# Output projection of an attention kernel: seven block products per slot in place of eight

## What is computed

```python
x = x + 0.5 * ffn(layernorm(x))
x = x + attn(layernorm(x))
x = x + 0.5 * ffn(layernorm(x))
# attn, shortened
q = rms_norm(x @ wq_a.T, q_norm_w) @ wq_b.T            # 32 heads, 128 + 64 (rotary)
kv_up = rms_norm(kv_c, kv_norm_w) @ wkv_b.T            # k_nope and v of each head
scores = (q_nope . k_nope + q_pe . k_pe) * scale       # causal
probs = softmax(scores)
out = (probs @ v).reshape(b, s, 32 * 128) @ wo.T
```

## Time and profile before

| | us |
|---|---|
| median of 3 runs (2258.32 to 2260.1) | 2259.83 |
| span of the profiled execution | 2257.3 |
| TensorE busy | 2213.3 (98%) |
| TensorE weight loads busy (beside the matmuls) | 1871.3 (83%) |
| VectorE busy | 1594.8 (71%) |
| ScalarE busy | 968.0 (43%) |
| GpSimd busy | 576.2 (26%) |

### The profile page before, as it was taken

How to read it: one execution, slowest core, us unless ns; L and a number is a source line. 1 busy time by engine, 2 the same in 40 slices (tenths; PEclk the granted TensorE clock), 3 DMA queues, 4 the chain that set the end, 5 groups by cost and what they waited for, 6 DMA issues and landing times.

```text
span 2257.3 us, 39455 instructions
## 1 busy us (share of the span) xinstructions
PE 2213.3 (98%) x11932; PEld 1871.3 (83%) x11932; DVE 1594.8 (71%) x3663; ACT 968.0 (43%) x2441; POOL 576.2 (26%) x642
## 2 busy tenths in 40 slices
PE   8989999999999999999999999999999999999998
PEld 7978888888888888887788988888888888888887
DVE  7656667776676766777787666766777766666777
ACT  6543444443444443443465534334344443334344
POOL 5312222122221222212144332222222222222212
PEclk9999999999999999999999999999999999999999
DMA  4023333332233333333423123333323333333321
GB/s 161 15 72 114 113 113 103 113 86 87 76 103 110 111 113 112 104 108 105 154 86 98 44 77 83 82 82 82 81 80 81 82 82 82 82 82 82 79 71 75
DMA packets 217433, 207.09 MB, mean 92 GB/s; under 512 B 144288, under 2 KB 172832, under 8 KB 215328
## 3 DMA queue, kind: packets, MB, share of 16 engines
q1 hardware_dynamic: 196928, 162.32, 25.7%
q10 hardware_dynamic: 20448, 44.04, 5.8%
HBM read 101.45 MB, written 54.53 MB: 69 GB/s over the span
## 4 chain that ended last, share of the span: by engine, by line
PE 88%; DVE 5%; issue 2%; DMA 2%; ACT 1%; POOL 1%; SPq 0%; ACTq 0%; DVEq 0%; POOLq 0%
PE ps L777 69%; PE ps L1141 6%; PE ps L856 4%; PE ps L1085 2%; PE ps L791 1%; PE ps L803 1%; DVE stage L2029 1%; DVE arena L1692 1%; PE ps L1092 1%; PE ps L1123 1%; ACT arena L1303 1%; DVE negmax L2019 1%; PE ps L805 1%; PE ps L1119 1%; DVE stats L1701 0%
## 5 line engine op out<-in xcount | busy, mean ns | idle before, releaser
L777 PE MATMUL ps<-arena 128*128 128x512 f32 x3264 | 876.9, 404 | 8.9 <-DVE xacc L1794 4.9
L1692 DVE TENSOR_TENSOR arena<-ps,arena 128x512 fp32r<-128x512 f32 (+2 forms) x920 | 538.4, 597 | 414.2 <-ACT arena L1303 414.0
L1303 ACT ACTIVATE arena<-ps 128x512 fp32r<-128x512 f32 (+2 forms) x920 | 471.8, 525 | 656.8 <-PE ps L777 429.6
L777 PEld LDWEIGHTS ps<-arena 128*128 128x128 f32 x3264 | 578.2, 188 | 119.6 <-issue 10.0
L777 PE MATMUL ps<-zT,arena 128*128 128x512 f32 (+1 forms) x1746 | 438.9, 395 | 1.7 <-DVE ropeT L1692 0.8
L1579 ACT ACTIVATE stage<-ps,negmax 128x128 f32<-128x128 f32 (+6 forms) x512 | 259.9, 508 | 368.3 <-DVE negmax L2019 360.6
L2041 DVE TENSOR_TENSOR xacc<-ps,xacc 128x512 f32<-128x512 f32 x512 | 350.0, 684 | 64.9 <-PE ps L777 58.3
L777 PEld LDWEIGHTS ps<-zT,arena 128*128 128x128 f32 x1746 | 320.2, 188 | 75.9 <-issue 5.6
L2278 POOL TENSOR_TENSOR stage<-stage,pos_tab 128x512 f32<-128x512 f32 (+1 forms) x66 | 83.3, 1262 | 973.7 <-ACT stage L1303 951.9
L777 PE MATMUL ps<-keyT,arena 128*128 128x192 f32 (+5 forms) x1152 | 267.7, 341 | 4.8 <-ACT stage L1579 4.6
L2019 DVE TENSOR_REDUCE negmax<-ps 128x1 f32<-128x128 f32 (+6 forms) x512 | 238.6, 466 | 17.6
(11 more groups left out here) (103 smaller groups left out, 1853.0 us busy)
## 6 DMA issues: line engine op xcount, KB each, us to landing
kept_out<-arena SPq DMA_DIRECT2D x16, 2048.0 KB, 6.4
arena<-arena SPq DMA_DIRECT2D x248, 128.0 KB, 3.0
arena<-kept_out ACTq DMA_DIRECT2D x30, 1024.0 KB, 5.9
stage<-in_wo SPq DMA_DIRECT2D x16, 1024.0 KB, 6.0
stage<-stage SPq DMA_DIRECT2D x248, 64.0 KB, 2.0
kept_q<-arena SPq DMA_DIRECT2D x16, 768.0 KB, 7.5
arena<-kept_q ACTq DMA_DIRECT2D x32, 384.0 KB, 3.4
out<-xacc SPq DMA_DIRECT2D x15, 512.0 KB, 2.7
```

The costliest lines, as they stand in the source:

```text
L777: last = nc.tensor.matmul(dst, w, m, start=start and n == 0, stop=stop and n == len(passes) - 1, skip_group_check=skip)
L1303: return nc.scalar.activation(dst, src, ACT.Copy)
L1692: return nc.vector.tensor_tensor(dst, src, part.bitcast(F32), ALU.subtract)
```

## The change

The output product of a unit is seen as a product of 2 x 2 blocks: token tile 0 or 1 of head 0 or 1 on the left (a11, a12, a21, a22), head by half of the width on the right (B11, B12, B21, B22). A form of Strassen's identity gives the four results from seven block products, with sums s1 to s4 on the left and T1 to T4 on the right.

- TensorE: `output` has seven products j of three matmuls. Some go on in the bank of an earlier one (start only for j = 0, 1, 3), and after each j VectorE adds the bank into `xacc`, seven adds per slot. Product j waits until the adds up to j - 2 are done.
- Left side, each slot: ScalarE copies the values raw (two copies), GpSimd makes s1, s2, s4, s3 and all low parts (`sums`), ScalarE makes the high parts in three groups (`split_a`). `o_split` is gone.
- Right side, p = 0: the m fills stay raw float32; GpSimd sums T1 to T4 (`sum_b`), ScalarE makes seven high parts, VectorE three low parts (B11, B21, B22) and GpSimd four (T1 to T4). 3.5 MB per group are kept and loaded again in p = 1, by SP (`keep_b`, `b_again`), one load for each product.
- The orders of the slots on all engines are changed, and `FILLS` with them: the pe fill now comes before score 2, the outputs in twos (0, 1), (2, 3), (4, 5) and 6, and 6 after `values`.
- Buffers are moved, several tables share one place, and two small tables are loaded again for p = 1.

```diff
         FILLS = [{
-            "front":  [None, None, "m2", None],
-            "output": [None, "q3", "m3", "w1"],
-            "second": [None, "m0", "pe0", "q0"],
-            "first":  ["pe1", None, None, None],
-            "third":  ["q2", None, "w0", "q1"],
-            "values": [None, "m1", None, None],
+            "front":  [None, "m3", None, None],
+            "output": ["pe1", "q2", "pe0", "q0"],
+            "second": ["m0", "m1", None, "w1"],
+            "first":  ["m2", "q3", "w0", "q1"],
         }] + [{
...
+        Y_OPS = ["a11", "a12", "s2", "s1", "s3", "a22", "s4"]
+        Y_NEW = [0, 1, 3]
+        Y_INTO = [(0, 0), (0, 0), (1, 0), (1, 1), (1, 1), (1, 0), (0, 1)]
+        B11, B21, T2, T1, T3, T4, B22 = range(NPROD)
+        RAW = {B11: "m0", B21: "m1", B22: "m3"}
...
+            def output(p, g, k, j, first):
...
                 if not (first and k == 2 and j < 2):
                     pe.wait_ge(y_added, n - 1)
...
-                for h in range(2):
-                    passes += three(oT[:, k % 2, 0, h, ts], oT[:, k % 2, 1, h, ts], w_out[:, h, 0, hs], w_out[:, h, 1, hs])
-                products(bank_y(j), passes).then_inc(y_done, 1)
+                a = [operand(Y_OPS[j], part) for part in range(2)]
+                products(bank_y(k, j), three(a[0], a[1], w_prod[:, j, 0], w_prod[:, j, 1]),
+                         start=j in Y_NEW, skip=True).then_inc(y_done, 1)
...
                 scores(p, g, k, 0, False, last)
                 scores(p, g, k, 1, False, last)
                 fills(p, g, k, "front", ev)
                 turn_probs(n, before, 0, False)
                 turn_probs(n, before, 1, False)
-                output(p, g, k, 0, False, last)
                 fills(p, g, k, "output", ev)
                 scores(p, g, k, 2, False, last)
                 turn_probs(n, before, 2, False)
-                output(p, g, k, 1, False, last)
+                out_(0, 1)
                 fills(p, g, k, "second", ev)
                 scores(p, g, k, 3, False, last)
+                out_(2, 3)
                 turn_probs(n, before, 3, False)
                 fills(p, g, k, "first", ev)
-                output(p, g, k, 2, False, last)
-                fills(p, g, k, "third", ev)
+                out_(4, 5)
                 values(n, before, False)
-                fills(p, g, k, "values", ev)
-                output(p, g, k, 3, False, last)
+                out_(6)
...
+                    m = unit_n(p, g, k)
                     apart(p, g, k)
                     fills(k, "front")
                     if k % 2 == 0:
                         turned(n, before, 0)
-                    exps(p, g, k, 0)
-                    if k % 2:
+                        exps(p, g, k, 0)
+                        turned(n, before, 1)
+                        split_a(m, 1)
                         exps(p, g, k, 1)
+                        split_a(m, 2)
+                    else:
+                        exps(p, g, k, 0)
                         turned(n, before, 0)
-                    turned(n, before, 1)
-                    if k % 2 == 0:
                         exps(p, g, k, 1)
+                        turned(n, before, 1)
+                        split_a(m, 1)
+                        split_a(m, 2)
+                    if k == 2 and p == 0:
+                        split_b(g, T3, last)
+                        split_b(g, T4, last)
                     fills(k, "output")
...
                     turned(n, before, 2)
                     exps(p, g, k, 2)
...
                 maxima(p, g, k, 2)
                 pt_split(n, before, 2)
-                y_add(p, g, k, 1)
+                adds(0, 1)
                 fills("second")
                 maxima(p, g, k, 3)
+                if k == 2 and p == 0:
+                    split_b(g, B22)
+                adds(2, 3)
                 pt_split(n, before, 3)
-                fills("first")
+                norms(p, g, k)
                 if early:
                     mom_early(g, k)
-                norms(p, g, k)
-                y_add(p, g, k, 2)
-                fills("third")
-                o_split(n, before)
-                fills("values")
-                y_add(p, g, k, 3)
+                fills("first")
+                adds(4, 5)
+                if k == 1 and p == 0:
+                    split_b(g, B11)
+                    split_b(g, B21)
+                adds(6)
...
+            def body(p, g, last=False):
+                ev = q_events(p, last)
+                sums(unit_n(p, g, 0), y_n(p, g, 0))
+                rotate(turns(p, g, 1), qbase(p, g) + ev["pe1"][0] + 1)
+                sums(unit_n(p, g, 1), y_n(p, g, 1))
+                if not last:
                     split_wpe(p, g + 1)
+                if p == 0:
+                    sum_b(g, 0, ("m2", "m3"), last)
+                    sum_b(g, 1, ("m0",), last)
+                    split_t(g, T1)
+                    sum_b(g, 2, ("m0", "m2"), last)
+                    sum_b(g, 3, ("m1",), last)
+                    split_t(g, T2)
+                sums(unit_n(p, g, 2), y_n(p, g, 2))
+                if p == 0:
+                    split_t(g, T3)
+                    split_t(g, T4)
                 if not last:
-                    rotate(turns(p, g, 1) + 1 + first, qbase(p, g) + ev["pe0"][0] + 1)
+                    rotate(turns(p, g, 1) + 1, qbase(p, g) + ev["pe0"][0] + 1)
+                sums(unit_n(p, g, 3), y_n(p, g, 3))
```

More of the change, by code:

```diff
@@ L142, in views, with two_names @@
             return cut
+        def views(name, size, dt):
+            return cutter(sb(name, [P, size], dt), size)
+        def two_names(name, size):
+            sb(name + "_place", [P, size])
+            at = nc.sbuf_base - 4 * size
+            return [cutter(nc.alloc_sbuf_tensor_at(name + part, [P, size], dt, offset=at), size)
+                    for part, dt in (("", F32R), ("_plain", F32))]
         W0 = 2 * KD * ZK
@@ L442, in build_macaron @@
         EV = [len(q_events(p, False)) for p in range(NPAIR)]
-        EVD = [n - 2 for n in EV]
+        EVD = [sum(name[0] in "qw" for name in q_events(p, False)) for p in range(NPAIR)]
         def qbase(p, g):
@@ L575, in first_body @@
                 if p > 0:
-                    for half in range(2):
-                        out_weights_back(sp, 0, half)
+                    for j in range(NPROD):
+                        b_again(0, j)
                 if p == 0:
@@ L640, in body @@
                 stack_halves(turns(p, g, 1), 1, 4 * slot_n(p, g, 0))
+                if p > 0:
+                    for j in range(NPROD):
+                        sp.wait_ge(y_done, y_n(p, g, 1) + j + 1)
+                        settle(sp)
+                        b_again(g, j)
                 if early:
@@ L1193, in slot, with out_ @@
                 ev = q_events(p, last)
+                def out_(*js):
+                    for j in js:
+                        output(p, g, k, j, False)
                 scores(p, g, k, 0, False, last)
@@ L1555, in read_fill @@
                 elif name[0] == "m":
-                    h, half = int(name[1]) % 2, int(name[1]) // 2
-                    if name in ("m0", "m2") and not first:
+                    if name == "m0" and not first:
                         act.wait_ge(wo_kept, 16 * g)
-                    dst, src = w_out[:, h, 0, half * HALF:(half + 1) * HALF], bank_m(name, first)
+                    dst, src = raw_at(name), bank_m(name, first)
                 else:
@@ L1632, in body @@
                         q_weights_back(g + 1, 1)
-                    valued(n, before)
-                    fills(k, "values")
-                    if k == 1 and p > 0:
-                        out_weights(p, g, 1)
+                    valued(n)
             def drained(p, s):
                 n = all_slots(p) - 1
-                for i in range(NS):
-                    turned(n, 3, i)
+                turned(n, 3, 0)
+                turned(n, 3, 1)
+                split_a(n - 1, 1)
+                split_a(n - 1, 2)
+                turned(n, 3, 2)
+                turned(n, 3, 3)
                 norm_ffn(s, 0)
@@ L2055, in fills, with adds @@
                         read_fill(p, g, name, ev)
+                def adds(*js):
+                    for j in js:
+                        y_add(p, g, k, j)
                 maxima(p, g, k, 0)
@@ L2063, in slot @@
                     maxima(p, g, k, 1)
-                y_add(p, g, k, 0)
                 fills("output")
@@ new lines, in split_t, with first_body @@
+            def split_t(g, j):
+                pool.wait_ge(b_hi, NPROD * g + B_ORDER.index(j) + 1)
+                settle(pool)
+                G.tensor_tensor(w_prod[:, j, 1], w_plain[:, j, 1], w_prod[:, j, 0].bitcast(F32),
+                                ALU.subtract).then_inc(t_lo, 1)
+            def first_body(p):
+                ev = q_events(p, False, True)
+                sums(unit_n(p, 0, 2), y_n(p, 0, 2) if p else None)
```

(4 more changed lines are left out.)

550 lines of the change are left out of this document (334 added, 216 removed).

## The result

| | before | after |
|---|---|---|
| median of 4 runs each, us | 2259.97 | 2420.16 |
| lowest and highest | 2258.32, 2260.79 | 2417.29, 2425.06 |
| span of the profiled execution | 2257.3 | 2419.6 |

What follows compares the result with a forecast made beforehand. The prediction took TensorE's instruction stream as the bound. A walk of the slots gave 2257.3 + 64 (p = 1) + 74 (p = 0) = 2395, and 2398 us as the runs' median, 2.5 over the profiled span; range 2235 to 2500.

Steps and rivals of the forecast that it cites:

- the likeliest case: Whole kernel slower, with GpSimd holding up some of VectorE's scales: 2330 to 2480 us, chance 0.50.
- Removed matmuls: TensorE's output: 21 matmuls per slot for 24, 0.71 us less per slot, 91 us over 32 groups.
- Product 2 behind ScalarE's order: Even slot: `split_a` and the pe read delay the turn 2 copy and VectorE's add; product 2 stalls 1.05 us.
- The lock: GpSimd and VectorE exclude each other by whole instructions; in even slots `norms` meets `rotate`, two waits, 2.2 us.
- Even slot 16.05: p = 1, k even: 13.85 us without GpSimd's exclusion plus 2.2 of waits at the scales, against 13.37 before.
- odd slot 14.9: p = 1, k odd: adds 4 and 5 end at 14.15, product 6 due at 13.7; a gain of 0.36 us.
- +4.3 per group: Group of four slots in p = 1: 61.9 us against 57.63; times 15 groups, +64 us.
- p = 0: +74 forecast: Group of four slots in p = 0, with the weights' work: 68.0 us against 63.10, +4.9, times 15 groups.
- First groups, drains and feed-forward at zero: Outside the looped groups: each loses 2.8 us of matmuls and gains the same waits, so no net change.
- DMAs at nothing: Seven loads per group, issued in slot 1, used over 10 us later, against 5.9 us per 1 MB load: no cost.
- Faster, the adds fall into VectorE's idle time: Rival: VectorE keeps up, its seven adds fitting its idle 30%; 2169 to 2255 us, chance 0.20.
- Slower without the lock: Rival: kernel slower, but GpSimd and VectorE don't exclude each other; 2262 to 2330 us, chance 0.18.

Runs made afterwards that it cites:

- b_order: The changed kernel with ScalarE's copy of turn 2 in even slots ahead of `split_a` and the pe read; 2401.2 us, ratio 1.062.
- a: The changed kernel with the last four GpSimd operations of each looped rotation on 64 of 512 columns, the rest left out; 2364.25 us, ratio 1.0458.
- c: The changed kernel with looped rotations cut to 64 columns and ScalarE's turn 2 copy moved earlier in even slots; 2316.05 us, ratio 1.0241.
- d: The kernel before, with only the pe fills of p = 1 moved ahead of score 2 in even slots; 2267.23 us, ratio 1.0027.
- h: The changed kernel with ScalarE's earlier turn 2 copy, and GpSimd's last four rotation operations held until the slot's scales are done; 2443.26 us, ratio 1.0813.
- j: As h, and in p = 0 GpSimd holds the right side from its second sum until the scales of k = 1 are done; 2459.4 us, ratio 1.0879.
- f1: The changed kernel with all looped scales of `norms` moved from VectorE to ScalarE, after the copy of turn 3; 2435.77 us, ratio 1.078.

## Why the prediction was right, and where it was not

The forecast was 2398 us, within 2235 to 2500; measured were 2420. The sign, the mechanism and the likeliest case held. Its terms:

- **Removed matmuls: right.** 2880 of the output form. The odd slot of p = 1, where little stands in the way, is 15.26 - 14.54 = 0.72 us shorter, against the 3 x 0.237 = 0.71 of the prediction.
- **Product 2 behind ScalarE's order: right in mechanism, a little too high.** 0.78 us of stall, 1.05 forecast. b_order takes it away; alone it is worth 19 us, with the rotation out of the way 48 (a to c).
- **The lock: shown, but its cost to the slot was taken at nearly twice its size.** Even slots' scales take 3.05 us where they take 0.97 alone, by two waits of about 1.1 us: +2.1 for +2.2 forecast; d shows it in the kernel before, and h, which keeps every operation whole, takes it away by the order of the two. The walk let all of the 2.2 land on product 6. In a the even slot is 14.4 us for 15.53, in h 13.60 for 14.78 in b: 1.1 to 1.2 us. The Trainium skill ("SBUF — State Buffer", section "SBUF: two separate sides") says that a VectorE operation in a two-port mode or with two SBUF inputs, the latter only against a GpSimd operation that reads SBUF, excludes and is excluded for the whole instruction. The trace agrees, and also for operations that read one input from PSUM, which that rule leaves free: low parts with both inputs in SBUF 1180 ns against 722, adds 682 ns against 684 in the kernel before.
- **Even slot 16.05: measured 15.53, in part by luck; odd slot 14.9: measured 14.54.** The walk began from 12.66 us of issue times and put 1.19 of waits on them, 13.85 without the lock. But a, which has the wait at product 2 and no lock, takes 14.4, and c and h, which have neither, 13.62 and 13.60. So the start of the sum was 0.9 too low, the waits 0.4 and the lock's share of the slot 1.0 too high, and these errors nearly cancel. Summed over 4 slots and 15 groups the 0.4 to 0.5 by which both walks ended too late are the miss in p = 1: +4.3 per group was forecast, +2.63 measured, so +39 in place of +64. Two slips in the working change nothing: the odd slot's issue times are 15.26 - 0.71 = 14.55, not 14.45 (measured 14.54), and with every scale waiting the walk's own terms give 2 x (13.85 + 4.4 + 14.9) = 66.3, not 66.1.
- **p = 0: +74 forecast, 15 x 5.85 = 88 measured.** By slots 15.60, 18.60, 19.37 and 15.20 us, for 16.05, 18.3, 18.0 and 15.6. The term that was too small is k = 2 (+1.4). ScalarE copies T3 and T4 (643.16) and reads the pe fill (644.21) before turn 2 (644.68), and product 2 stands 2.79 us:

```profile
643.16 1.14 ACT L1353 ACTIVATE arena<-arena_plain 128x512 fp32r<-128x512 f32 x2
...
644.21 0.58 ACT L1353 ACTIVATE stage<-ps 128x512 f32<-128x512 f32 x1
644.68 0.59 ACT L1353 ACTIVATE arena<-ps 128x512 fp32r<-128x512 f32 x1
...
645.30 0.69 DVE L1798 TENSOR_TENSOR arena<-ps,arena 128x512 fp32r<-128x512 f32 x1 [2.42 <-ACT arena L1353]
...
646.65 2.04 PE L835 MATMUL ps<-arena,extra 128*128 128x512 f32 x6 [2.79 <-DVE xacc L2151]
```

  T3 and T4 ahead of that copy were in the prediction's walk; B22's low part comes at 647.90, after the stall. After such a stall the granted clock is low for a while, 0.51 between 647.90 and 651.30 (of 1 at 2.4 GHz, so 1.2 GHz). That is not what makes k = 2 long. In the slot of the group before, from 567.30, product 2 stands 2.78 us and the clock stays at 1.00; there TensorE then stands 1.23 at product 6, which it doesn't where the clock was low, and the slot is 19.37 us too. Of the twelve k = 2 slots between the two issues nine have such a stretch, and only two of these are longer, 20.68 and 20.64, where it began only 0.2 to 0.3 us after product 2 had started.
- **First groups, drains and feed-forward at zero: wrong, about +35 us.** This is the largest error of the sum, and it was hidden in the total: p = 1 came out 25 too high, p = 0 14 too low, this 35 too low. That the total was only 22 us off is luck in that part. The prediction argued that 2.8 us of matmuls saved would pay for the waits. About 9 of the 35 us are the first group of p = 1 with its 7.30 us wait, a path that the prediction didn't walk. A granted clock below full is another part: in the windows of 100 us from 1100 to 1300 it is 0.93 and 0.95 of 2.4 GHz, where the kernel before has 1.00 in each window of 100 us from 900 to 1400. Over the three stretches outside the 12 + 12 groups (260, 418 and 195 us long) it is 0.97, 0.96 and 0.98 (0.99, 1.00 and 1.00 before), which is worth at most some 25 us by an estimate from these shares, and less where TensorE would have waited anyway. How the rest divides was not tried.
- **DMAs at nothing: right.** Each of the seven loads lands in 4.8 us (median), and no wait on them is among the causes of TensorE's idle time.
- **Rivals.** *Faster, the adds fall into VectorE's idle time* fails: VectorE is at 78% and TensorE waits for it 137 us. *Slower without the lock* fails by d, h and the 3.05 us. GpSimd as a queue I had only as an addition to one rival, 0.85 us per odd slot if the rotation delays the sums. In the changed kernel it costs nothing (the sums start 0.19 us before the odd slot), but h pays 2.9 us there (17.41 for 14.54). GpSimd's work fits as time (53%), but none of the orders tried keeps rotation, sums and scales all off the path; that there is none is not shown.

## What to carry to other kernels

Before adding an operation with two SBUF inputs to GpSimd, look which in-place or two-input VectorE operations run at that moment, and price both orders: beside them it costs on VectorE, after them it costs whoever reads GpSimd's next result. A removed matmul pays only where the engine that frees its bank has no wait in front of it; walk the slot in each engine's queue order, check the sum of issue times against a slot that really ran without waits, and walk the first and last groups too, since a term left at zero there was the largest error here. When two waits guard successive deadlines, take both away at once before you say what either is worth (104 us together, 75 apart).

## What the runs showed of the hardware

- The exclusion between GpSimd and VectorE is per instruction and does not cost both alike: four scales of 128 columns went from 0.97 to 3.05 us, while the rotation's operations beside them went from 1.29 to 1.38 in that slot. The long instructions lose little; of the short ones every second waits for a long one (0.29, 1.32, 0.31, 1.38 us, where one alone takes 0.25).
- The low parts of VectorE with both inputs in SBUF are held up too, wherever GpSimd's stream lay: 722 ns without its stream, 1180, 1373, 1459 and 1539 ns with it in the changed kernel, h, c and j.
- ScalarE's scales, at the same time as the rotation, were not held up (f1): four in 1.44 us from 1705.88, beside a GpSimd operation of 1.30 us from 1705.94.
- After product 2 had stood 2.8 us the granted clock fell to 1.2 GHz in nine of twelve slots, and in seven of the nine it cost nothing, since TensorE would otherwise have waited for VectorE at product 6.
